# A pre-norm block on one core: the second batch's down products in 16-bit parts, and the chain for their unit rebuilt and moved

## What is computed

```python
q  = x1 @ W_q.T ; kv = x1 @ W_kv.T             # x1 = layernorm(x), 16 heads of 32
qf, kvf = fft(q) / norm, fft(kv) / norm        # per head
kvf = cumsum(kvf, axis=1)                      # along the rows of a batch
x = x + real(ifft(qf * kvf)) @ W_o.T
x2 = layernorm(x)
gate = silu((x2 @ fp8(gate_w)) * gate_scale)
up   = (x2 @ fp8(up_w)) * up_scale
x = x + ((gate * up) @ fp8(down_w)) * down_scale      # 512 -> 1536 -> 512
```

## Time and profile before

| | |
|---|---|
| median of 3 runs | 420.11 us (420.07 to 420.39) |
| the profiled execution | 419.79 us, span 418.0 us |
| busy: PE, DVE | 408.8, 297.4 us |
| busy: ACT, POOL | 193.2, 108.2 us |
| granted TensorE clock | 0.996 |
| 16-bit down products, 32-bit down products | 184 and 192 matmuls |

### The profile page before, as it was taken

How to read it: one execution, slowest core, us unless ns; L and a number is a source line. 1 busy time by engine, 2 the same in 40 slices (tenths; PEclk the granted TensorE clock), 3 DMA queues, 4 the chain that set the end, 5 groups by cost and what they waited for, 6 DMA issues and landing times.

```text
span 418.0 us, 5504 instructions
## 1 busy us (share of the span) xinstructions
PE 408.8 (98%) x1897; PEld 202.8 (49%) x1897; DVE 297.4 (71%) x514; ACT 193.2 (46%) x323; POOL 108.2 (26%) x114
## 2 busy tenths in 40 slices
PE   7999999999999999999999999999999999999994
PEld 3744454445555554454555555454444444444442
DVE  4998998999999699997984972167865854422234
ACT  3687756587736245445242563255442441131220
POOL 0133551015154137043541012032461001300003
PEclk9999999999999999999999999999999999999998
DMA  8986546600181143232112014411112051200002
GB/s 249 264 267 239 163 117 162 149 17 2 38 256 36 26 77 71 57 127 74 28 26 50 2 29 101 72 50 53 26 26 52 0 77 25 100 2 0 2 0 101
DMA packets 57547, 33.55 MB, mean 80 GB/s; under 512 B 49456, under 2 KB 49840, under 8 KB 57392
## 3 DMA queue, kind: packets, MB, share of 16 engines
q1 hardware_dynamic: 57088, 32.93, 30.3%
q10 hardware_dynamic: 432, 0.28, 0.2%
HBM read 17.44 MB, written 4.19 MB: 52 GB/s over the span
## 4 chain that ended last, share of the span: by engine, by line
PE 89%; DMA 3%; DVE 3%; ACT 2%; POOL 1%; SPq 1%; issue 1%; POOLq 0%; DVEq 0%
PE bd L488 20%; PE bu L470 19%; PE bg L470 19%; PE ba L370 14%; PE ba L415 8%; PE bd L370 3%; DMA h<-x_dram 1%; PE ba L388 1%; PE bd L415 1%; DMA hT<-w_q_dram 1%; PE bd L388 1%; PE bd L356 1%; PE bu L415 1%; POOL xs L1603 1%; PE bg L447 0%
## 5 line engine op out<-in xcount | busy, mean ns | idle before, releaser
L470 PE MATMUL bu<-hT,gu 128*128 128x512 f16 x384 | 90.7, 379 | 0.0
L470 PE MATMUL bg<-hT,gu 128*128 128x512 f16 x376 | 89.0, 379 | 0.0
L1234 DVE SCALAR_TENSOR_TENSOR ff<-bu,us,sl 128x512 f32<-128x512 f32 x48 | 35.9, 748 | 56.0 <-PE bu L470 52.8
L741 ACT ACTIVATE sl<-bg,gs 128x512 f32<-128x512 f32 x48 | 32.9, 686 | 78.0 <-PE bg L470 77.0
L370 PE MATMUL ba<-wf,xT 128*128 128x512 f16 x288 | 63.2, 379 | 0.0
L470 PEld LDWEIGHTS bu<-hT,gu 128*128 128x128 f16 x384 | 37.5, 98 | 45.5 <-DVE ff L1234 0.6
L470 PEld LDWEIGHTS bg<-hT,gu 128*128 128x128 f16 x376 | 35.6, 98 | 44.9 <-issue 4.1
L488 PE MATMUL bd<-dw,fu 128*128 128x512 f32 x192 | 51.1, 411 | 0.0
L1634 POOL TENSOR_TENSOR h<-ff,h 128x512 f32<-128x512 f32 x14 | 17.5, 1272 | 122.2 <-DVE ff L1265 122.2
L370 PEld LDWEIGHTS ba<-wf,xT 128*128 128x128 f16 x288 | 27.9, 98 | 34.1 <-issue 1.1
L488 PE MATMUL bd<-own,half 128*128 128x512 f16 x184 | 43.0, 379 | 0.0
(11 more groups left out here) (201 smaller groups left out, 524.3 us busy)
## 6 DMA issues: line engine op xcount, KB each, us to landing
h<-x_dram SPq DMA_DIRECT2D x16, 256.0 KB, 4.2
out_dram<-h SPq DMA_DIRECT2D x15, 256.0 KB, 2.0
hT<-w_q_dram SPq DMA_DIRECT2D x4, 256.0 KB, 5.0
gu<-w_kv_dram SPq DMA_DIRECT2D x4, 256.0 KB, 4.4
hT<-gate_w_dram SPq DMA_DIRECT2D x2, 512.0 KB, 3.5
hT<-up_w_dram SPq DMA_DIRECT2D x2, 512.0 KB, 5.6
gu<-woT_dram SPq DMA_DIRECT2D x1, 1024.0 KB, 5.1
hT<-down_w_dram SPq DMA_DIRECT2D x2, 512.0 KB, 4.9
```

Source lines behind the costliest of these rows:

```text
L470: m = e.matmul(bk[:, :], gu[:, c, 4 * w + k, col:col + P], hT[:, b % 2, part, k, :], start=k == 0 and part == 0, stop=k == KT - 1 and part ...
L741: e.activation(sl[:, n % 2, :], bg[:, :], ACT.Silu, scale=gs[:, i:i + 1]).then_inc(a_silu, 1)
L1234: e.scalar_tensor_tensor(out=ff[:, n % 2, :], in0=bu[:, :], scalar=(us if b < HALF else us2)[:, i:i + 1], in1=sl[:, n % 2, :], op0=ALU.mul ...
```

## The change

`HALF` becomes 1: batch 1 too uses `dw16`, `fu16`, `us2` and `ds2`. The maxima stay at the start of batch 1. The bound product moves ahead of `pe_qk(2, 3, 1)`, right behind `pe_down(11)`, and takes another bank. `act_bound` is gone: instead of a root, `dve_unit2` halves exponents by shifts of the bits. It moves ahead of `dve_f(12)`, with the sum of qk(2, 2, 1) before it. Output 0 of batch 0 is scaled after `dve_fu(12)` instead of before. `ds2` is made in `dve_unit_out`, after `dve_f(13)`. `act_fu(12)` gets a wait for the last rounded weights.

```diff
-HALF = 2
+HALF = 1
@@ tenancies
-        order += [("qk", b, t, w) for t in (1, 2, 3) for w in range(2)]
-        if b == HALF:
+        order += [("qk", b, t, w) for t in (1, 2) for w in range(2)] + [("qk", b, 3, 0)]
+        if b == HALF + 1:
             order += [("bound",)]
+        order += [("qk", b, 3, 1)]
@@ emptied
             if kind == "bound":
-                return a_bound, 1
+                return v_unit2, 1
@@ tensor_program
                 pe_down(e, b * NI - 1)
+                if b == HALF:
+                    pe_bound(e)
                 if nxt < NB:
                     pe_qk(e, nxt, 3, 1)
-                if nxt == HALF:
-                    pe_bound(e)
@@ scalar
-        def act_bound(e):
-            e.wait_ge(s_bound, 1)
-            e.activation(bound[:, 3:6], ba[AT["bound",]][:, 0:3], ACT.Sqrt).then_inc(a_bound, 1)
@@ act_fu
+            if n == HALF * NI:
+                e.wait_ge(*rounded(17))
@@ dve_unit2
-            e.wait_ge(a_bound, 1)
-            e.tensor_tensor(bound[:, 9:10], bound[:, 3:4], bound[:, 4:5], ALU.mult).then_inc(v_unit2, 1)
+            e.wait_ge(s_bound, 1)
+            e.tensor_copy(bound[:, 3:6], ba[AT["bound",]][:, 0:3]).then_inc(v_unit2, 1)
             e.wait_ge(v_unit2, 1)
-            e.tensor_tensor(bound[:, 10:11], bound[:, 9:10], bound[:, 5:6], ALU.mult).then_inc(v_unit2, 1)
-            e.wait_ge(v_unit2, 2)
-            e.tensor_scalar(bound[:, 11:12], bound[:, 10:11], 2.0 ** -3, 1e-30, ALU.mult, ALU.max).then_inc(v_unit2, 1)
+            e.tensor_scalar(bound[:, 9:10], bound[:, 3:4], bound[:, 4:5], 1e-30, ALU.mult, ALU.max).then_inc(v_unit2, 1)
+            e.tensor_scalar(bound[:, 10:11], bound[:, 5:6], 1e-30, None, ALU.max).then_inc(v_unit2, 1)
             e.wait_ge(v_unit2, 3)
-            e.tensor_scalar(bound[:, 12:13].bitcast(I32), bound[:, 11:12].bitcast(I32), 0x7F800000, None,
-                            ALU.bitwise_and).then_inc(v_unit2, 1)
+            e.tensor_scalar(bound[:, 11:13].bitcast(I32), bound[:, 9:11].bitcast(I32), 24, 23,
+                            ALU.logical_shift_right, ALU.logical_shift_left).then_inc(v_unit2, 1)
             e.wait_ge(v_unit2, 4)
-            e.reciprocal(bound[:, 13:14], bound[:, 12:13]).then_inc(v_unit2, 1)
+            e.tensor_scalar(bound[:, 13:14], bound[:, 11:12], 2.0 ** 125, bound[:, 12:13], ALU.mult,
+                            ALU.mult).then_inc(v_unit2, 1)
             e.wait_ge(v_unit2, 5)
-            e.tensor_scalar(us2[:, :], us[:, :], bound[:, 13:14], None, ALU.mult).then_inc(v_unit2, 1)
+            e.reciprocal(bound[:, 14:15], bound[:, 13:14]).then_inc(v_unit2, 1)
+            e.wait_ge(v_unit2, 6)
+            e.tensor_scalar(us2[:, :], us[:, :], bound[:, 14:15], None, ALU.mult).then_inc(v_unit2, 1)
+
+        def dve_unit_out(e):
             e.wait_ge(*rounded(17))
-            e.tensor_scalar(ds2, ds[:, :], bound[:, 12:13], None, ALU.mult).then_inc(v_unit2, 1)
+            e.tensor_scalar(ds2, ds[:, :], bound[:, 13:14], None, ALU.mult).then_inc(v_unit2, 1)
@@ dve_f
             if n == HALF * NI:
-                e.wait_ge(v_unit2, 6)
+                e.wait_ge(v_unit2, 7)
@@ vector_program, start of batch b
                     dve_most(e, 2, 1)
                     dve_gus(e)
+                    dve_sum(e, nxt, 2, 1)
+                    dve_unit2(e)
                 dve_f(e, b * NI)
-                dve_scale_out(e, b - 1, 0)
+                if b > HALF:
+                    dve_scale_out(e, b - 1, 0)
                 dve_fu(e, b * NI)
-                if nxt < NB:
+                if b == HALF:
+                    dve_scale_out(e, b - 1, 0)
+                elif nxt < NB:
                     dve_sum(e, nxt, 2, 1)
                 dve_scale_out(e, b - 1, 1)
...
                 dve_f(e, b * NI + 1)
+                if b == HALF:
+                    dve_unit_out(e)
                 if nxt < NB:
                     dve_norm_tail(e, nxt, range(NT))
...
                 dve_fu(e, b * NI + 3)
-                if nxt == HALF:
-                    dve_unit2(e)
@@ gpsimd_program
-                if b + 1 == HALF:
+                if b == HALF:
                     for n in range(NI // 2):
                         pool_dw(e, n)
```

More of the change, by code:

```diff
@@ L197, in build @@
         a_zh, v_zl = sem("act_zh"), sem("dve_zl")
-        v_most, s_bound, a_bound, v_unit2, v_gus, p_dw = (
-            sem(n) for n in ("dve_most", "pe_bound", "act_bound", "dve_unit2", "dve_gus", "pool_dw"))
+        v_most, s_bound, v_unit2, v_gus, p_dw = (
+            sem(n) for n in ("dve_most", "pe_bound", "dve_unit2", "dve_gus", "pool_dw"))
         d_cst, d_cst2, d_id, d_wo, d_sc, d_carry = (sem("d_" + n) for n in ("cst", "cst2", "id", "wo", "sc", "carry"))
@@ L950, in scalar_program @@
                     act_sqrt1(e, nxt, range(NT))
-                if nxt == HALF:
-                    act_bound(e)
-                if nxt < NB:
                     act_ks(e, nxt, 0)
@@ L1252, in dve_scale_out @@
             if b == HALF and t == 0:
-                e.wait_ge(v_unit2, 7)
+                e.wait_ge(v_unit2, 8)
             if b < NB - 1:
```

## The result

The kernel after takes 422.24 us in the median of 7 executions (420.65 to 423.12); before, run beside it, takes 420.03 (419.14 to 420.39, 7). The ratio is 1.006, with a 95% interval from 1.0045 to 1.0074: slower by 2.5 us (1.9 to 3.1). The forecast was 421.3 (420.3 to 423.0) and slower.

What follows compares the result with a forecast made beforehand. PE was taken to bound the kernel, except for the chain without slack to tri at a batch's start. 2.62 - 1.33 - 0.13 = +1.16 gave 420.95 profiled, 421.27 against the median; range 420.3 to 423.0.

Steps and rivals of the forecast that it cites:

- The delay of tri(2, 0): Start of batch 1: the moved unit chain makes DVE's norm tail, and so PE's tri, late by 2.62 us.
- `dve_unit_out`: Between `dve_f(13)` and the norm tail: blocked beside POOL's fourth add, it holds DVE 0.74 us; 0.40 if free.
- The gain of the products: Batch 1's down products 12 to 23 in 16-bit: 1.33 us for 13 to 22, 0.13 for 23, together 1.46.
- they do in batch 2 with the same work: DVE, ACT and POOL keep up with a faster PE in batch 1, so the 1.33 us are really had.
- the prediction's own sign: The gain is wrong if tri(2, 0) to the first matmul after batch 1 isn't 60.3 to 60.8 us.
- Rival 1: PE's clock falls to 1.2 GHz in the new gap at tri(2, 0): +1.5 us, so 422.8; chance 0.20.
- the forecast's case: Tri(2, 0) is delayed 2.3 to 3.1 us against 1.46 of gain: 421.3, own range 420.9 to 421.8; chance 0.52.
- Rival 2: DVE runs batch 1's regrouped start without idle time, reciprocal at 187.9 or less: faster, 418.5; chance 0.08.
- Rival 3: `dve_unit_out` finds ports free, small operations are quick: tri(2, 0) 1.8 to 2.2 late, 420.65; chance 0.13.
- Rival 4: Batch 3's x tile lands 1 us later than reckoned, so down 13 waits: 422.0; chance 0.04.
- Rival 5: Half-precision down products in batch 1 gain nothing: +2.6 us, 422.7; chance 0.03.
- what I costed at nothing: POOL's six casts, removing `act_bound` and the old unit chain, the wait for round 17, bound's other bank: no cost.

Runs made afterwards that it cites:

- the chain alone: Kernel after with batch 1's down products taking 32-bit parts again, unit, its chain and all orders kept: 424.53 us, ratio 1.0123 to before.
- the longer gap: Kernel after plus one unused 2.28 us DVE reduction before `dve_unit_out`, so PE waits longer ahead of tri(2, 0): 425.91 us, ratio 1.0156 to before.
- the first kernel: Kernel before with 16-bit down products in batch 1, and no unit or chain for it there: 418.52 us, ratio 0.9973 to before.

## Why the prediction was right, step by step

- **The delay of tri(2, 0)**: forecast +2.62, measured +2.75. From down 11's start, forecast against measured: `dve_f(12)` +3.7, +3.89; `dve_fu(12)` +5.1, +5.34; POOL's first add +6.5, +6.72; `dve_f(13)` +10.3, +10.59; the reciprocal +11.7, +11.88. The early 0.2 is in the small operations (1.53 from the copy to f(12), forecast 1.3); the rest follows at the forecast pace. The copy of three columns out of PSUM took 0.16, the small end that I took, and `dve_fu(12)` 0.69 instead of 1.80, as forecast.
- **`dve_unit_out`**: forecast 0.74, measured 0.63 in the timeline and 0.61 by moving it away. The mechanism, waiting for the add that runs, holds: in all ten profiles in which it met an operation of POOL it ended 0.28 to 0.29 behind that operation's end, with lengths from 0.54 to 1.40. The Trainium skill (SBUF — State Buffer, on the shared port pair) has the second one block for the other's whole length. The trace agrees up to 0.2 us: after a block to the recorded end, 189.56, its own 0.48 would end at 190.04, and it ended at 189.84. Whether POOL lets go 0.2 early or its recorded ends are that rough, no run shows.
- **The gain of the products**: forecast 1.46, measured 1.18 alone, and 0.85 in the change (0.70 from tri to batch 3's qk, 0.15 at down 23). The step that failed is "they do in batch 2 with the same work": PE, DVE, ACT and POOL do keep up, but I had left the DMA out, and o(2, 1) waits for a transpose that takes longer than in batch 2. By the prediction's own sign the gain was wrong: the stretch from tri is 61.17, not 60.3 to 60.8. Of the 0.63, 0.31 come with the products alone and 0.32 with the chain alone, both at o(2, 1). The term was 0.6 too large in the change, the delay 0.1 too small, which makes +1.9 of +1.16.
- **Rival 1, the clock**, had 0.20, and happens in half of the executions. Its price was right: forecast 1.5, measured 1.42 in a profile and 1.6 between the groups. Its time, 422.8, is nearer to the median than the forecast's. Over the whole stretch of the profile the fall costs 1.16, as a shorter wait at o(2, 1) gives some back. The Trainium skill (TensorE: Matmul & The Clock Gate, on the two states) treats the low state as the one that activity lifts; the traces agree, for the clock comes back while PE is dense, 3.4 us after the fall here and 6.8 with the longer gap. So the forecast's case is true of the executions without the fall (421.44, 1.4 above before's 420.03, though the profile without a fall has +1.90: the executions of one kernel spread over more than that difference), and rival 1 of the others. That the median of 422.24 lies in the stated range is in part luck: it is above the forecast's own 420.9 to 421.8, and the range reached it because it was widened for a rival that had 0.20. The delay was right on its own; the gain was not.
- **Rival 2** was wrong: the reciprocal came at 189.77, not at 187.9. **Rival 3** too: tri was 2.75 late, not 1.8 to 2.2. **Rival 4**: `dve_stats1(3, 0)` starts at 192.33 without a wait. **Rival 5** is excluded by the first kernel. Nothing of what I costed at nothing turned up, but for the transposes' DMA.
- Down 12's fourth tile waited 0.39, forecast 0.3, and was swallowed.

## What to carry to other kernels

Where a cheap chain must run once before a batch, count who stands behind it in the engine's written order: the seven small operations cost 1.5, and the bound product in front of them, which stands behind down 11, as much again, so that f was 3.0 late. Behind f, 1.1 came back, as `dve_fu(12)` no longer met an add, but the ring of two tiles and `dve_unit_out` took most of it again: 2.75 at tri, more than the shorter products gave back. A gap of 2.3 to 2.4 us in a dense matmul stream brought the clock's fall here in about half of the executions, one of 4.4 in all five, at 1.2 to 2 us each, so price it, and know that one profile can miss it. A stretch that "runs the same list" in another batch is a bound for the engines only: compare the DMA's landing times as well.

## What the runs showed of the hardware

- The same gap of 2.43 and 2.44 us gave a clock of 1.00 behind it in one execution, and 0.50 for 3.4 us in another. With matmuls of unused results in the gap the mean clock was 0.996 to 1.0 in 12 executions, where the longer gap alone gave 0.990 to 0.994.
- A DVE tensor_scalar of 128x512 took 0.48 alone. Started while a tensor_tensor of POOL ran, it ended 0.28 to 0.29 us behind POOL's end in ten profiles, and took 0.54, 0.70 or 1.40 by how early it had started. A small one took 0.78 beside POOL and, with POOL idle, 0.23.
- 1088 transpose packets of the same 0.26 MB took between 25.0% and 55.4% of the DMA engines' time in 5 us, and landed 2.5 to 3.8 us after issue.
